# Post-norm decoder of two layers: the transfer of the shift rows moved from SP's instruction row to ScalarE's

## Chip, cores and metric

The kernel runs on one core of one Trainium2 chip. The metric is the device time of one execution in microseconds; the time of a kernel is the median of its runs. Three runs of the kernel before gave 3743.16, 3737.08 and 3737.75 us, so the median is 3737.75.

## The reference

Two decoder layers, each with `x = layernorm(x + f(x))` three times, for 16 sequences of 256 tokens, 128 features, 16 heads of 8. Layer 0 has self-attention, cross-attention to a context of 1601 keys of 96 features, and a mixture of experts. Layer 1 has a state-space layer, the same cross-attention with other weights, and a feed-forward net. The part that matters here is attention:

```python
scores = jnp.einsum('bqhd,bkhd->bhqk', q, k) * scale
weights = jax.nn.softmax(scores, axis=-1)
out = jnp.einsum('bhqk,bkhd->bqhd', weights, v).reshape(B, Lq, D)
return out @ w_o + b_o
```

## The kernel before

One function, `attention` (L158), builds each of the three attention stages (self, cross0, cross1); experts, the state-space layer and the feed-forward net stand between and after them. A program stage is written by hand for each engine, in one row of instructions per engine, and the engines meet through semaphores.

**Work of one batch.** Heads are taken in four quads of four heads (`g` 0 to 3). A product in full precision is made from bf16 parts: queries and keys are split into three bf16 parts each (`SPLIT_Q`, `SPLIT_K`, on GpSimd after the first batch, L277 to L283), and SP copies the parts, row by row, into stacked tiles `Q` and `K` (in self-attention one tile `QK`) by nine transfers at a time: `STACK_Q` (L348) once per batch, `STACK_K` (L361) once per quad in the cross stages, and once per batch in self-attention (L364). `LOAD_C` and `LOAD_X` (L333) fetch the inputs of a later batch.

For each quad the softmax needs the maximum of every query's scores first. TensorE computes scores for it (operation A, L486 and L493, into one of two ring buffers), VectorE takes the maxima (L663, L668, L672) into `nm`, GpSimd splits them in three bf16 parts (L407 to L413) into `mp`, TensorE transposes them (operation MT, L502), and ScalarE copies the transposed shift rows from PSUM to `mst` (L586, 32 x 256 bf16). Then one DMA, operation ROWS (L370), moves them as 64 short rows (16 KB) into the last rows of the stacked `Q` tile. There they take part in the second score product, so that exp gets the score less its maximum.

Operation B (L520) computes that product of scores, in slots of two units of two heads; ScalarE takes the exponentials (L600) into `Pr`; PV (L539) multiplies with the values into `oT`; after a quad, EV (L608) copies `oT` to `OTs`. At the end of a batch come the division (OX), two matmuls (ONT, OUT), and the layer norm. B of quad `g` begins with a wait for that quad's rows:

```python
if cp == 0 and pk == 0:
    pe.wait_ge(max_rows[g], 16 * (b + 1))
```

The score banks `sT` are three; B of a slot waits for the first exponential of the slot before it. GpSimd (before it writes `mp` again) and ScalarE (before it writes `mst` again) wait for the rows of the quad two before.

**The order of the work.** `_schedule` (L76) gives every operation a slot number, relative to its batch; `plan` sorts the operations of a pass by slot, then by rank (B, A, PV, MT, then all others), then by batch. Every engine walks through the same plan and issues what is its own, so each engine's order is fixed. A cross batch has 56 slots, 14 per quad (`u`); a self batch has 8, 2 per quad. In the cross stages:

```python
out += [(g * u - 4, ("MT", g)), (g * u - 3, ("ROWS", g))]
```

and in self-attention both stand in one slot, `g * u - 5`, MT first, and EV of the quad whose turn it is ahead of ROWS. In the cross stages the last two slots of a quad are short: they have one chunk of 65 keys in place of two chunks of 128. `STACK_K` for the next batch is scheduled at slots 27, 30, 44 and 57, `STACK_Q` at 12, `LOAD_C` at 27; the first of the `STACK_K` waits only for the split of the keys, the others also for the quad's last B.

On SP every operation stands behind the one ahead of it, so that a wait of one holds all that follow. ROWS waits there for ScalarE's copy: `read` (L133) gives the count of ScalarE's ring semaphore at which MT's buffer has been read. ScalarE's own row holds, per slot, the exponentials of B (two per slot), the copies of MT, EV, XT and ONT, and one issue of two DMAs for the feed-forward weights (`ffn_load`, L1455), behind the first XT of the second cross stage.

Of the kernel before, what the change touches and what calls it, by code (L numbers as in the profile page):

```python
# [13 lines left out]
P = 128  # L14
B, S, D = 16, 256, 128
H, DH = 16, 8
# [10 lines left out]
ROWS = P // 2  # L27
PASSES = (((0, 0), (0, 1), (1, 0), (1, 1), (0, 2)), ((2, 0), (1, 2), (2, 1), (2, 2)))
SHIFT = len(PASSES[1])
# [128 lines left out]
def attention(nc, top, cfg, X, ident_f, ident_b, src_T, wts, x_dram=None, ffn_weights=None):  # L158

    n = cfg.name  # L160
    with ExitStack() as ctx:
        def sb(name, shape, dt):
            return ctx.enter_context(nc.sbuf_tensor(f"{n}_{name}", shape, dt))
# [4 lines left out]
        def sem(name):  # L168
            return top.enter_context(nc.semaphore(f"{n}_{name}"))
# [19 lines left out]
        if cfg.cross:  # L189
            qparts = sb("qparts", [D, PARTS, S], BF16)  # L190
            kparts = sb("kparts", [D, PARTS, NKP], BF16)
            Qs = [sb(f"Q{j}", [P, PAIRS, 2, S], BF16) for j in range(cfg.qbufs)]
            Ks = [sb(f"K{j}", [P, PAIRS, 2, NKP], BF16) for j in range(cfg.kbufs)]
        else:
# [3 lines left out]
            Qs, Ks = ([T[:, :, :, k, :].rearrange("p t a n -> p a t n") for T in stacks] for k in range(2))  # L198
# [6 lines left out]
        mst = sb("mst", [2 * DH * 2, 2, S], BF16)  # L205
# [26 lines left out]
        by = {"dve": sem("ring_dve"), "act": sem("ring_act")}  # L232
# [6 lines left out]
        max_rows = [sem(f"max_rows{g}") for g in range(QUADS)]  # L239
# [18 lines left out]
        def rows(c):  # L258
            return cfg.chunks[c][1]
# [56 lines left out]
        @block.sync  # L316
        def _(sp):

            for dst, w in ((wq, "wq"), (wk, "wk"), (wv, "wv"), (wo, "wo")):
                n_in = wts[w].shape[0] // 16 * 16  # L320
                sp.dma_start(dst[0:n_in, :], wts[w][0:n_in]).then_inc(w_loaded, 16)
                if n_in < wts[w].shape[0]:
                    sp.dma_start(dst[n_in:, :], wts[w][n_in:]).then_inc(w_loaded, 16)
            sp.dma_start(bq[:, :], wts["bq"].rearrange("(p o) -> p o", o=1)).then_inc(w_loaded, 16)
            sp.dma_start(bo[:, :], wts["bo"].partition_broadcast(P)).then_inc(w_loaded, 16)

            for i in iterations:
                for op, ix, off in cfg.plan(i):
                    b = i + off
                    if op in ("LOAD_X", "LOAD_C"):  # L330
                        if b >= 2:
                            sp.wait_ge(by["dve"], cfg.read(i, "V", (len(cfg.chunk_units) - 1,), off - 2))
                        sp.dma_start(sT_in[b % 2][0:KIN, :], src_T[b]).then_inc(in_ready[b % 2], 16)  # L333
                        if x_dram is not None and b < 2:
                            n = NT // 2
                            sp.dma_start(X[:, b * n:(b + 1) * n, :],
                                         x_dram.rearrange("b (t p) f -> p (b t) f", p=P)[:, b * n:(b + 1) * n, :])\
                              .then_inc(x_in, 16)
                    elif op == "STACK_Q":
                        if b == 0:  # L340
                            sp.wait_ge(rows_set, cfg.qbufs)
                        if b >= cfg.qbufs:
                            sp.wait_ge(scored, NB * (b - cfg.qbufs + 1))
                        sp.wait_ge(split_q, SQ * (b + 1))
                        Q = Qs[b % cfg.qbufs]
                        for t, pairs in enumerate(PASSES):
                            for r, (a, _) in enumerate(pairs):
                                sp.dma_start(Q[r:P:DH, :, t, :], qparts[:, a, :]).then_inc(stacked_q, 16)  # L348
                    elif op == "STACK_K":
                        g = ix[0]  # L350
                        if b == 0:
                            sp.wait_ge(rows_set, cfg.qbufs + cfg.kbufs)

                        if b >= cfg.kbufs and not (cfg.cross and g == 0):
                            sp.wait_ge(scored, NB * (b - cfg.kbufs) + NB // cfg.kgroups * (g + 1))
                        if g == 0:
                            sp.wait_ge(split_k, SK * (b + 1))
                        for t, pairs in enumerate(PASSES):
                            for r, (qa, ka) in enumerate(pairs):
                                if cfg.cross:  # L360
                                    sp.dma_start(Ks[0][r:P:DH, g * KG:(g + 1) * KG, t, 0:NK],  # L361
                                                 kparts[g * KP:(g + 1) * KP, ka, 0:NK]).then_inc(stacked_k[g], 16)
                                else:
                                    sp.dma_start(stacks[b % cfg.kbufs][r:P:DH, t, :, :, :],  # L364
                                                 parts[:, qa:PARTS + ka + 1:PARTS + ka - qa, :])\
                                      .then_inc(stacked_k[0], 16)
                    elif op == "ROWS":
                        g = ix[0]
                        sp.wait_ge(by["act"], cfg.read(i, "MT", (g,), off))
                        sp.dma_start(Qs[b % cfg.qbufs][SHIFT:P:DH, 2 * g:2 * g + 2, 1, :], mst[:, g % 2, :])\  # L370
                          .then_inc(max_rows[g], 16)

        @block.gpsimd
        def _(pool):
# [190 lines left out]
        @block.scalar  # L565
        def _(act):
            act.wait_ge(w_ready, READY)

            for i in iterations:
                k = 0  # L570
                for op, ix, off in cfg.plan(i):
                    b = i + off
                    if op in cfg.reader:
                        R = ring[:, cfg.parity(i, k), :]
                        if cfg.reader[op] == "act":
                            act.wait_ge(filled, cfg.base(i, None) + k + 1)
                        k += 1
                    if op == "XT":
                        act.activation(xT[:, :], R[:, 0:S], ACT.Copy).then_inc(by["act"], 1)
                        if ffn_weights is not None and b == 0:  # L580
                            ffn_load(ffn_weights, act)
                    elif op == "MT":
                        g = ix[0]
                        if b * QUADS + g >= 2:
                            act.wait_ge(max_rows[(g + 2) % QUADS], 16 * (b + g // 2))
                        act.activation(mst[:, g % 2, :], R[0:4 * DH, 0:P].bitcast(BF16), ACT.Copy)\  # L586
                           .then_inc(by["act"], 1)
                    elif op == "B":
                        g, cp, pk = ix
                        for j in range(2):  # L590
                            u = g * UQ + 4 * cp + 2 * pk + j
                            act.wait_ge(scored, b * NB + u + 1)
                            if b * NB + u >= NPR:
                                was = (u - NPR) % NB
                                last = min(was % UQ // 4 * 2 + 1, NCHK - 1)
                                done = was // UQ * NV + 1 + [last in cs for cs in cfg.bursts].index(True)
                                act.wait_ge(weighed, b * NW + done - (NW if u < NPR else 0))
                            nc_ = min(2, NCHK - 2 * cp)
                            r = rows(2 * cp)
                            act.activation(Pr[0:r, u % NPR, 0:nc_ * S], sT[0:r, cfg.sT_bank(b, u), 0:nc_ * S],  # L600
                                           ACT.Exp).then_inc(exped, 1)
                    elif op == "EV":
                        g = ix[0]
                        gq = b * QUADS + g
                        act.wait_ge(weighed, (gq + 1) * NV)
                        if b > 0:
                            act.wait_ge(by["dve"], cfg.read(i, "OX", (g // 2,), off - 1))
                        act.activation(OTs[:, g, :], oT[:, 0:S], ACT.Copy).then_inc(o_out, 1)  # L608
                    elif op == "ONT":
                        act.activation(OnT[:, :], R[:, 0:S], ACT.Copy).then_inc(by["act"], 1)  # L610
# [844 lines left out]
def ffn_load(fw, act):  # L1455
    weights, lora = fw.dram
    act.dma_start(fw.raw[:, :, :], weights).then_inc(fw.loaded, 16)
    act.dma_start(fw.lora[:, :], lora).then_inc(fw.lora_loaded, 16)
# [270 lines left out]
```

## Time and profile before

| What | Value |
|---|---|
| Median of three runs | 3737.75 us |
| Profiled execution, its own time | 3738.05 us |
| Its span in the profile | 3736.1 us |
| Busy: PE, DVE, ACT, POOL | 3416.9, 2878.3, 2312.5, 1182.9 us |
| ROWS transfers | 64 in self-attention, 128 in the two cross stages |
| Self-attention | to about 330 us of the span |
| Cross stages | about 330 to 1732 us and 2260 to 3661 us |

PE is TensorE's matmul row, PEld its weight loads, DVE VectorE, ACT ScalarE, POOL GpSimd, SP the sync engine. A name with a q behind it, as SPq or ACTq, is that engine's instruction sequencer, where DMA issues stand; the time of such an issue is the time that it holds the sequencer, and its landing is counted from the start of the issue until its semaphore is full. In a timeline a row gives start and duration in us, engine, line, operation, output and inputs, and in brackets the idle time ahead of it with what ended it. Neighbouring instructions of a group are merged to one row, with their number behind the x.

### The profile page before, as it was taken

How to read it: one execution, taken by the hardware profiler on the slowest of the kernel's cores; microseconds unless marked ns; L12 is line 12 of the kernel's file. 1: busy time of each engine (PE TensorE's matmuls, PEld its weight loads, DVE VectorE, ACT ScalarE, POOL GpSimd, SP SyncE). 2: the span in 40 equal slices, each digit the busy share in tenths (PEclk: the TensorE clock that was granted, in tenths of full speed). 3: DMA queues.
4: the chain of work that ended last, by engine and by line, in shares of the span. 5: the costliest groups of instructions: out<-in, count | busy, mean ns of one | idle time of the engine just before them, and what ended most of it. 6: DMA issues, size and time to landing. Idle time of an engine off the chain costs nothing. (4 is left out here: it accounts for less than half of the span.)

```text
span 3736.1 us, 96496 instructions
## 1 busy us (share of the span) xinstructions
PE 3416.9 (91%) x38874; PEld 1684.4 (45%) x38874; DVE 2878.3 (77%) x3902; ACT 2312.5 (62%) x4560; POOL 1182.9 (32%) x1918
## 2 busy tenths in 40 slices
PE   6885999999999999998999684999999999999998
PEld 3442444444444444445676582444444444444445
DVE  5776788888888888885644996888888888888874
ACT  3663677777777767675333531677777777677773
POOL 5552222232222222212765263332222222332202
PEclk9997999999999999998999896999999999999999
DMA  4222222222322222220000002222322222222310
GB/s 102 76 74 68 55 63 57 57 59 56 71 66 65 55 63 57 56 47 27 1 1 2 1 1 69 61 56 62 75 59 62 55 65 55 61 56 61 69 22 24
DMA packets 159093, 195.26 MB, mean 52 GB/s; under 512 B 31268, under 2 KB 117288, under 8 KB 158392
## 3 DMA queue, kind: packets, MB, share of 16 engines
q1 hardware_dynamic: 158472, 188.49, 21.4%
q8 instruction: 307, 5.03, 0.6%
q14 instruction: 138, 1.13, 0.1%
q10 hardware_dynamic: 176, 0.61, 0.1%
HBM read 27.95 MB, written 2.10 MB: 8 GB/s over the span
## 5 line engine op out<-in xcount | busy, mean ns | idle before, releaser
L600 ACT ACTIVATE cross_Pr<-cross_sT 128x512 f32<-128x512 f32 (+1 forms) x3584 | 1833.6, 563 | 766.7 <-PE cross_sT L520 765.7
L663 DVE TENSOR_REDUCE cross_nm<-cross_ring 128x2 f32<-128x802 f32 x2048 | 1975.0, 991 | 321.1 <-PE cross_ring L486 292.6
L520 PE MATMUL cross_sT<-cross_Q,cross_K 64*128 64x256 bf16 x13312 | 1043.4, 273 | 47.8 <-ACT cross_Pr L600 42.1
L539 PE MATMUL cross_oT<-cross_Pr,cross_V 128*9 128x256 f32 x13312 | 1030.3, 381 | 0.0
L520 PEld LDWEIGHTS cross_sT<-cross_Q,cross_K 64*128 64x128 bf16 x13312 | 511.4, 95 | 769.1 <-ACT cross_Pr L600 636.7
L486 PE MATMUL cross_ring<-cross_K,cross_Q 64*128 64x401 bf16 x4096 | 661.9, 336 | 62.5 <-DMA cross_K<-cross_kparts 33.5
L407 POOL TENSOR_TENSOR cross_mp<-cross_nm,cross_one 128x8 bf16<-128x8 f32 x128 | 25.9, 202 | 1371.8 <-DVE cross_nm L668 1371.8
L539 PEld LDWEIGHTS cross_oT<-cross_Pr,cross_V 128*9 128x9 f32 x13312 | 198.2, 88 | 412.2 <-issue 245.7
L486 PEld LDWEIGHTS cross_ring<-cross_K,cross_Q 64*128 64x128 bf16 x4096 | 199.1, 94 | 203.2 <-DVE cross_nm L663 107.5
L967 ACT ACTIVATE moe_r<-moe_bank 128x512 f32<-128x512 f32 x144 | 85.9, 597 | 188.6 <-PE moe_bank L894 187.2
L857 POOL TENSOR_TENSOR moe_hh<-moe_r,moe_rc 128x512 f32<-128x512 f32 x128 | 169.1, 1326 | 88.2 <-DVE moe_rc L1089 87.5
L600 ACT ACTIVATE self_Pr<-self_sT 128x512 f32<-128x512 f32 x256 | 138.8, 594 | 85.0 <-PE self_sT L520 84.7
L672 DVE TENSOR_REDUCE self_nm<-self_ring 128x4 f32<-128x1024 f32 x128 | 155.3, 1223 | 46.7 <-PE self_ring L493 44.0
L1089 DVE TENSOR_TENSOR moe_rc<-moe_r,moe_bank 128x512 f32<-128x512 f32 x128 | 87.5, 686 | 131.0 <-PE moe_bank L907 130.4
L917 PEld LDWEIGHTS moe_bank<-moe_down,moe_hh 128*128 128x128 f32 x1152 | 150.6, 192 | 54.4 <-issue 40.8
L1245 PE MATMUL ssm_bank<-ssm_diag,ssm_state 128*128 128x128 f32 x1024 | 130.9, 291 | 46.4 <-DVE ssm_state L1366 46.4
L277 POOL TENSOR_TENSOR cross_qparts<-cross_qf,cross_one 128x256 bf16<-128x256 f32 x30 | 18.4, 612 | 485.2 <-DVE cross_qf L640 485.2
L917 PE MATMUL moe_bank<-moe_down,moe_hh 128*128 128x128 f32 x1152 | 152.6, 275 | 1.4 <-POOL moe_hh L857 1.2
L894 PE MATMUL moe_bank<-moe_xT,moe_up 128*128 128x512 f32 x288 | 148.5, 600 | 1.0 <-ACT moe_s L949 1.0
L1366 DVE TENSOR_TENSOR_SCAN ssm_state<-ssm_decay,ssm_dtu 128x2048 f32<-128x2048 f32 x32 | 145.8, 4603 | 4.5 <-ACT ssm_decay L1293 4.4
L1245 PEld LDWEIGHTS ssm_bank<-ssm_diag,ssm_state 128*128 128x128 f32 x1024 | 125.7, 204 | 51.5 <-DVE ssm_state L1366 51.4
L470 PE MATMUL cross_ring<-cross_wv,cross_in 97*128 97x128 f32 (+1 forms) x832 | 124.1, 296 | 21.0 <-DVE cross_nm L663 21.0
(272 smaller groups left out, 3075.2 us busy)
## 6 DMA issues: line engine op xcount, KB each, us to landing
cross_K<-cross_kparts SPq DMA_DIRECT2D x1152, 100.1 KB, 2.3
cross_in<-in_ctx_T_dram SPq DMA_DIRECT2D x32, 600.4 KB, 5.6
self_QK<-self_parts SPq DMA_DIRECT2D x144, 128.0 KB, 2.8
cross_Q<-cross_qparts SPq DMA_DIRECT2D x288, 64.0 KB, 2.1
self_in<-in_x_T_dram SPq DMA_DIRECT2D x16, 128.0 KB, 2.2
cross_Q<-cross_mst SPq DMA_DIRECT2D x128, 16.0 KB, 1.8
out_dram<-X SPq DMA_DIRECT2D x8, 256.0 KB, 2.3
moe_up<-in_moe_up_dram SPq DMA_DIRECT2D x1, 1152.0 KB, 6.0
```

The costliest lines, as they stand in the source:

```text
L470: mm = pe.matmul(R[0:r, (c - lo) * D:(c - lo + 1) * D], sT_in[b % 2][:, s:s + r], wv[:, :], start=True, stop=True)
L486: mm = pe.matmul(R[:, 512 * j:512 * j + cfg.block], Q[ROWS * j:ROWS * (j + 1), pair, 0, t * P:(t + 1) * P], K[ROWS * j:ROWS * (j + 1), pai ...
L520: mm = pe.matmul(sT[0:r, cfg.sT_bank(b, u + j), (c % 2) * S:(c % 2 + 1) * S], K[ROWS * j:ROWS * (j + 1), pair, t, s:s + r], Q[ROWS * j:ROW ...
L539: mm = pe.matmul(oT[32 * j:32 * j + VR, 0:S], V[0:r, b % VB, c, 4 * g + j, :], Pr[0:r, slot, (c % 2) * S:(c % 2 + 1) * S], start=(c == 0), ...
L600: act.activation(Pr[0:r, u % NPR, 0:nc_ * S], sT[0:r, cfg.sT_bank(b, u), 0:nc_ * S], ACT.Exp).then_inc(exped, 1)
L663: dve.tensor_reduce(nm4[:, g % 2, t, :, pk, blk], R.rearrange("p (j n) -> p j n", j=2)[:, :, 0:cfg.block], AX.X, ALU.max, negate=True).the ...
L672: dve.tensor_reduce(nm[:, g % 2, :, :, a].rearrange("p t j -> p j t"), R.rearrange("p (j t n) -> p j t n", j=2, t=QT), AX.X, ALU.max, nega ...
L857: pool.tensor_tensor(hh[:, s, :], r[:, s, :], rc[:, s, :], ALU.mult).then_inc(hidden, 1)
L894: pe.matmul(bank[:, n % UPS, :], up[:, m, :], xT[:, i * BLK:(i + 1) * BLK], start=True, stop=True)\
L917: mm = pe.matmul(bank[:, 5 + i % 2, t * D:(t + 1) * D], hh[:, n % BUFS, t * P:(t + 1) * P], down[:, m, :], start=(first and t == 0), stop= ...
L1245: return pe.matmul(bank[:, tile // BT, (tile % BT) * D:(tile % BT + 1) * D], lhs, rhs, start=first and tile % BT == 0, stop=True, skip_gro ...
L1366: dve.tensor_tensor_scan(state[:, k % BUFS, :], decay[:, k % BUFS, :], dtu[:, h * HALF:(h + 1) * HALF], 0.0, ALU.mult, ALU.add).then_inc(s ...
```

## The change

ROWS is taken out of SP's program and put into ScalarE's, at the same place of the same plan, with the same wait, semaphore, source and destination. Nothing else changes.

```diff
--- before.py
+++ after.py
@@ -364,11 +364,6 @@
                                     sp.dma_start(stacks[b % cfg.kbufs][r:P:DH, t, :, :, :],
                                                  parts[:, qa:PARTS + ka + 1:PARTS + ka - qa, :])\
                                       .then_inc(stacked_k[0], 16)
-                    elif op == "ROWS":
-                        g = ix[0]
-                        sp.wait_ge(by["act"], cfg.read(i, "MT", (g,), off))
-                        sp.dma_start(Qs[b % cfg.qbufs][SHIFT:P:DH, 2 * g:2 * g + 2, 1, :], mst[:, g % 2, :])\
-                          .then_inc(max_rows[g], 16)
 
@@ -585,6 +580,11 @@
                         act.activation(mst[:, g % 2, :], R[0:4 * DH, 0:P].bitcast(BF16), ACT.Copy)\
                            .then_inc(by["act"], 1)
+                    elif op == "ROWS":
+                        g = ix[0]
+                        act.wait_ge(by["act"], cfg.read(i, "MT", (g,), off))
+                        act.dma_start(Qs[b % cfg.qbufs][SHIFT:P:DH, 2 * g:2 * g + 2, 1, :], mst[:, g % 2, :])\
+                           .then_inc(max_rows[g], 16)
                     elif op == "B":
```

## Rows read from the trace of the kernel before

**Rows 1.** The page, busy us of each engine, share of the span and instructions.

```profile
PE 3416.9 (91%) x38874; PEld 1684.4 (45%) x38874; DVE 2878.3 (77%) x3902; ACT 2312.5 (62%) x4560; POOL 1182.9 (32%) x1918
```

**Rows 2.** Busy time by stretch: self-attention, and 470 us of cross0.

```profile
30.00:320.00 290.00, 237.07 (x2958) 134.61 (x2958) 204.51 (x339) 178.67 (x396) 144.25 (x410) 1.00 0.29 72
...
430.00:900.00 470.00, 456.81 (x5719) 197.70 (x5715) 389.57 (x490) 335.99 (x684) 110.12 (x204) 1.00 0.28 64
```

**Rows 3.** Timeline, cross0: two long slots in a row.

```profile
1028.94 0.61 PE L520 MATMUL cross_sT<-cross_Q,cross_K 64*128 64x256 bf16 x8
...
1029.59 1.08 ACT L600 ACTIVATE cross_Pr<-cross_sT 128x512 f32<-128x512 f32 x2 [0.21 <-PE cross_sT L520]
...
1030.24 0.61 PE L520 MATMUL cross_sT<-cross_Q,cross_K 64*128 64x256 bf16 x8
```

**Rows 4.** Timeline, cross0: around the ROWS of quad 2, short slots behind it.

```profile
1016.08 0.56 SPq L370 DMA_DIRECT2D cross_Q<-cross_mst  x1
1016.22 1.08 ACT L600 ACTIVATE cross_Pr<-cross_sT 128x512 f32<-128x512 f32 x2 [0.17 <-PE cross_sT L520]
...
1017.53 0.65 ACT L600 ACTIVATE cross_Pr<-cross_sT 65x256 f32<-65x256 f32 x2 [0.22 <-PE cross_sT L520]
...
1018.14 0.41 PE L520 MATMUL cross_sT<-cross_Q,cross_K 64*65 64x256 bf16 x4
...
1019.20 0.61 PE L520 MATMUL cross_sT<-cross_Q,cross_K 64*128 64x256 bf16 x8
```

**Rows 5.** Waits, 60 to 300 us: engine, line, waited for, us, times, longest.

```profile
ACT self_Pr L600 <- PE self_sT L520: 78.1, 64, 2.2
...
PE self_sT L520 <- ACT self_Pr L600: 6.5, 14, 0.5
```

**Rows 6.** ROWS by its tile and line: duration in ns, who waited, landing.

```profile
L370 SPq DMA_DIRECT2D cross_Q<-cross_mst x128: 539/540/563, 381.8 to 3633.9; - x128
...
  POOL self_mp L407: 76.2, 14
  PEld cross_sT L520: 6.0, 9
  PE cross_sT L520: 1.6, 5
...
DMA to landing us min/median/max: 1.7/1.8/3.7
```

**Rows 7.** Timeline, start of self-attention: a transpose MT.

```profile
54.24 0.27 PE L502 MATMUL self_ring<-ident_b,self_mp 128*32 128x128 bf16 x2 [0.88 <-POOL self_mp L413]
```

**Rows 8.** Timeline, start of cross1: a DMA issue behind a copy on ScalarE.

```profile
2267.78 0.38 ACT L579 ACTIVATE cross_xT<-cross_ring 128x256 f32<-128x256 f32 x1 [35.78 <-PE cross_ring L448]
2267.80 0.38 ACTq L1457 DMA_DIRECT2D ffn_raw<-in_L_ffn_weights_T_dram  x1
```

**Rows 9.** Timeline, self-attention: around one ROWS.

```profile
150.21 0.54 SPq L370 DMA_DIRECT2D self_QK<-self_mst  x1
...
150.35 1.08 ACT L600 ACTIVATE self_Pr<-self_sT 128x512 f32<-128x512 f32 x2
...
151.00 0.61 PE L520 MATMUL self_sT<-self_QK 64*128 64x256 bf16 x8 [0.47 <-ACT self_Pr L600]
...
151.76 1.05 PE L539 MATMUL self_oT<-self_Pr,self_V 128*9 128x256 f32 x16
...
153.11 0.29 PE L502 MATMUL self_ring<-ident_b,self_mp 128*32 128x128 bf16 x2 [0.29 <-DVE self_nm L672]
```

**Rows 10.** Last key split, SP's stack and load behind it; landings before, behind the load.

```profile
1009.93 0.30 POOL L283 TENSOR_TENSOR cross_kparts<-cross_res,cross_kparts 128x65 bf16<-128x65 f32 x1
...
1023.57 0.59 SPq L333 DMA_DIRECT2D cross_in<-in_ctx_T_dram  x1
...
cross_K<-cross_kparts SPq DMA_DIRECT2D x9, 100.1 KB, 2.3
...
cross_K<-cross_kparts SPq DMA_DIRECT2D x9, 100.1 KB, 4.2
```

## Prediction, made before the changed kernel was run

> **What bounds the kernel now.** Start with the page's busy line and the table by stage. TensorE is busy for 91% of the span, yet it isn't the whole story: in the first cross-attention stage, 430 to 900 us, PE, DVE and ACT are busy 457, 390 and 336 of 470 us [rows 1, 2]. Busy PE time is modelled, so the bound has to be read from the order of instructions. The timeline of one quiet slot shows a loop. The score matmuls (B) take 0.61 us. ScalarE starts two exponentials 0.04 us after their end, 1.08 us for the two. The next B starts 1.30 us after the one before, about 0.11 us after the first exponential ends. The sum 0.61 + 0.04 + 0.54 + 0.11 is 1.30 [rows 3]. So it is this handoff between PE and ACT that sets the time of a long slot. ScalarE has 0.21 us of idle time in each slot, before its next first exponential; a delay of ScalarE below that costs nothing, and one above it goes straight into the loop. The two slots after the one with ROWS are short (65 keys). The exponentials at 1017.53 last 0.65 us for two, so the first ends at 1017.86; with the same 0.11 us B could start at 1017.97, but it starts at 1018.14 [rows 4]. There PE has something else to finish, and ScalarE has 0.17 us more to spare.
>
> The stage of self-attention is looser: PE, DVE and ACT are busy 237, 205 and 179 of 290 us, and ScalarE waits for PE far more often than PE for ScalarE: from 60 to 300 us it is 78.1 against 6.5 us, and of these last waits there is about one per batch (14 in this stretch) [rows 2, 5].
>
> **What the change moves.** ROWS is one DMA of 16 KB per quad: 64 in self-attention, 128 in the two cross stages. Each holds SP for 0.54 us and lands 1.8 us after its issue. Waits of others for it: POOL 76.2 us, but PE only 6.0 us before weight loads and 1.6 us before matmuls [rows 6]. After the change the same 192 issues stand in ScalarE's own row, each behind a wait for ScalarE's own copy; nothing is computed less.
>
> **Gain on SP.** In self-attention one ROWS per batch sits behind nine stack transfers, and the POOL split, which waits for an earlier row to land, loses 76.2 us so, in 14 waits [rows 6]. But POOL is ahead of need: from 60 to 300 us no wait of PE for the POOL split stands in the list of waits, in which PE's 6.5 us for ScalarE do [rows 5]. Where nobody waits, its end is worth nothing. In the start-up a late row does reach PE: the transpose MT waits 0.88 us for the split [rows 7]. I take 0.9 us. In the cross stages, PE's waits on the rows are 7.6 us in all, in single places where a landing takes up to 3.7 us against a median of 1.8 [rows 6]. A different issuer has no reason to cure those; I take 0, with 7.6 us as the bound, so that the gain ends near 9 us.
>
> **Cost on ScalarE, cross stages (128 issues).** No row shows ROWS on ScalarE; the nearest is the load of the FFN weights. There ScalarE's copy starts at 2267.78 and lasts 0.38 us, and the DMA issue behind it starts at 2267.80 and takes 0.38 us [rows 8]. So the issue starts 0.02 us after the activation ahead of it has started, and runs beside it. ROWS is one slot after MT, so its wait is long fulfilled. Put it behind the second exponential of its slot: pair at 1016.22, second at about 1016.76, issue 1016.78 to 1017.32 (0.54, SP's duration for this shape), while the exponential ends at 1017.30 and the next is not due before 1017.53 [rows 4]. That leaves 0.21 us in which ScalarE must be ready again, and 0.17 us in the short slot behind it. Cost 0. If that cover failed, each 0.1 us beyond it would be 128 x 0.1 = 13 us.
>
> **Cost in self-attention (64 issues).** Here ROWS stands in MT's own slot, so ScalarE must wait until its copy is through. SP, which waits for the same copy, issues at 150.21, and at 150.35 ScalarE's next exponentials start [rows 9]. On ScalarE the issue would run from 150.21 to 150.75 and push those exponentials by 0.40 us. Queued behind the issue: the exponentials; waiting for them: B at 151.00, where PE waits 0.47 us now. This wait stands about once per batch. At the other quads ScalarE waits for PE, on average 78.1 / 64 = 1.2 us [rows 5], and the same 0.40 us vanish in it. B goes to 151.40 and PV from 151.76 to 152.16, ending at 153.21 instead of 152.81; MT, released at 153.11 by DVE, is late by 0.10 us [rows 9]. I take 16 x 0.10 = 1.6 us. Ends: nothing, or all 64 x 0.40 = 26 us.
>
> **Rows land later.** In the cross stages SP issues at 1016.08, ScalarE at 1016.78, and B of the next quad starts at 1019.20 [rows 4]: 2.42 us against a landing of 1.8, a reserve of 0.6 us, and no wait. SP changes too. The nine stack transfers of keys for the next batch, now held behind ROWS until 1016.64, depend only on the last POOL split, done at 1010.23. They would run from 1010.3 to 1016 or 1017, and the context load, now at 1023.57, would follow at once, in the same microsecond as ScalarE's ROWS [rows 4, 10]. What a load does to a neighbour: keys that land in 2.3 us land in 4.2 us right behind it [rows 10], 1.9 us more. That is behind it in one queue. If ROWS paid the whole of it, it would miss B by 1.9 - 0.6 = 1.3 us, in one quad of each of some 30 batches: 39 us. As ROWS is in another queue and small, I take 0 and keep 39 as the bound. The Trainium skill (DMA: Bandwidth & Descriptors, Queues, rings and completion order) says that each DMA engine takes turns between its queues packet by packet; by that ROWS waits for single packets of the load and not for its end. No row here shows two busy queues at once.
>
> **The sum.** -0.9 (start-up) + 1.6 (self-attention) + 0 + 0 = about +1 us on the profiled execution, 3738.05 us (span 3736.1 and 1.95 around it), which stands 0.3 us above the median of 3737.75. That gives 3739 us, no change. A measurement of this kernel can tell some 0.2%, 7.5 us.
>
> **Rival 1, slower: the issue isn't hidden.** The next exponentials would start only after the issue, and the issue after the second exponential's end, or take longer on ScalarE. Against it speaks the pair at 2267.78 [rows 8]; for it, that no activation follows there that would show when ScalarE is ready again. Place: the slot of ROWS. Price: issue from 1017.30 to 1017.84, next exponentials 0.3 us late, 0.1 to 0.3 us of it left after the short slot, x128 = 13 to 38 us; in self-attention 16 x 0.5 = 8 us. Time 3760 to 3785, middle 3772. It decides from an issue over 0.75 us, or as soon as ScalarE needs over 0.2 us to resume.
>
> **Rival 2, slower: self-attention doesn't absorb.** The 0.40 us count at more quads than one: 32 to 64 x 0.40 gives 13 to 26 us, 3751 to 3764. Against it: 78.1 us of ScalarE waiting for PE [rows 5].
>
> **Rival 3, slower: rows late beside the context load.** Up to 39 us as above; a half is more probable, 3758.
>
> **Rival 4, faster: SP was a bottleneck.** The 7.6 us of waits and the start-up's come back, and perhaps something of POOL's 76.2 us: 3729 to 3731. Against it: PE doesn't wait for those rows in any regular slot.
>
> That the change doesn't do what it says is improbable: the issue simply moves, and ACT's queue must show it.
>
> **Chances.** Forecast 0.60; rival 1 0.16; rival 2 0.06; rival 3 0.08; rival 4 0.10. Faster by over 0.2% 0.09, within 0.62, slower 0.29. Alone the forecast would have 3734 to 3745. For 8 in 10 the range reaches down to 3730 and up, into rival 1, to 3774.
>
> **What would show it.** Right: 192 DMA issues on ACT's queue of 0.54 us, starting 0.02 us after the second exponential; the gap after them at 0.2 us; 1.30 us slots; the wait of POOL on self_mst nearly gone; the keys' stack at 1010; landings of 1.8 to 2.4 us. Wrong: exponentials after ROWS that had been waiting for "issue" rather than PE (rival 1), PE L520 waiting on the rows' DMA once per batch (rival 3), or a cross stage whose first exponentials and maxima all come over 8 us later (rival 2).

## The result, and the profile after

Four runs of the changed kernel took 3790.85 to 3796.22 us, median 3791.72; four of the kernel before, beside them, 3737.08 to 3743.16, median 3738.44. The ratio is 1.0141, 95% interval 1.0129 to 1.0154: the change costs 53 us. The forecast was no change, 3739 us, and the range ended at 3774, so it was wrong in the time and in the range.

The profiled execution spans 3789.5 us (mean granted clock 0.964) against 3736.1 (0.973), 53.4 us more. From SP's first load of each stage, the stages became longer by 2.6 us (self-attention, its end at 330.2, now 332.8), 23.8 us (cross0, 1401.9 to 1425.7), 1.9 us (MoE and SSM), 25.9 us (cross1, 1401.1 to 1427.0) and -0.8 us (FFN). First the busy line and the queues of the page (columns of a queue: packets, MB, share of the 16 DMA engines):

```profile
PE 3436.7 (91%) x38874; PEld 1694.8 (45%) x38874; DVE 2879.0 (76%) x3902; ACT 2318.7 (61%) x4560; POOL 1183.1 (31%) x1918
...
q1 hardware_dynamic: 149256, 185.33, 20.8%
...
q10 hardware_dynamic: 9392, 3.76, 0.4%
```

The counts are those of [rows 1]. ACT's busy time has grown by 6 us of 3789, which excludes a slower ScalarE. PE's grew by 20 us with the same instructions, which asks for the clock. q10 is ScalarE's DMA queue and holds the rows now: the issue has moved as the diff says. Next comes ROWS by its tile: issue durations in ns (min/median/max), the engines that waited, in us and times, and the landing:

```profile
L586 ACTq DMA_DIRECT2D cross_Q<-cross_mst x128: 542/551/587, 384.4 to 3687.6; - x128
...
  PEld cross_sT L515: 46.8, 23
  PE cross_sT L515: 35.5, 18
...
DMA to landing us min/median/max: 1.7/1.8/6.1
```

Beside [rows 6], the issue and the median landing are as they were. But the longest landing went from 3.7 to 6.1 us, and PE's waits for the rows from 1.6 to 35.5 us. So it is a few transfers that are very late. The timeline shows one (waits in brackets):

```profile
1108.88 0.58 SPq L333 DMA_DIRECT2D cross_in<-in_ctx_T_dram  x1
1109.14 0.60 ACT L600 ACTIVATE cross_Pr<-cross_sT 128x512 f32<-128x512 f32 x1 [0.17 <-PE cross_sT L515]
1109.23 0.54 ACTq L586 DMA_DIRECT2D cross_Q<-cross_mst  x1
1109.63 0.59 ACT L600 ACTIVATE cross_Pr<-cross_sT 128x512 f32<-128x512 f32 x1
...
1110.45 0.65 ACT L600 ACTIVATE cross_Pr<-cross_sT 65x256 f32<-65x256 f32 x2 [0.22 <-PE cross_sT L515]
...
1114.36 0.61 PE L515 MATMUL cross_sT<-cross_Q,cross_K 64*128 64x256 bf16 x8 [2.17 <-DMA cross_Q<-cross_mst]
1115.00 1.08 ACT L600 ACTIVATE cross_Pr<-cross_sT 128x512 f32<-128x512 f32 x2 [2.85 <-PE cross_sT L515]
```

SP's context load is issued 0.35 us ahead of ROWS. The next long score matmul B stands still for 2.17 us, and behind it ScalarE for 2.85. The DMA view of 1108 to 1117 us gives KB each and microseconds to landing:

```profile
cross_in<-in_ctx_T_dram SPq DMA_DIRECT2D x1, 600.4 KB, 5.1
cross_Q<-cross_mst ACTq DMA_DIRECT2D x1, 16.0 KB, 5.1
```

16 KB on a queue of their own take as long as the 600 KB ahead of them. SP's own view tells how the load got there (start, time of all issues of the group):

```profile
1019.14 6.07 SPq L361 DMA_DIRECT2D cross_K<-cross_kparts  x9
1025.25 0.58 SPq L333 DMA_DIRECT2D cross_in<-in_ctx_T_dram  x1
...
1103.18 5.66 SPq L361 DMA_DIRECT2D cross_K<-cross_kparts  x9
1108.88 0.58 SPq L333 DMA_DIRECT2D cross_in<-in_ctx_T_dram  x1
```

In the kernel before, the same queue read:

```profile
1016.08 0.56 SPq L370 DMA_DIRECT2D cross_Q<-cross_mst  x1
1016.69 6.84 SPq L361 DMA_DIRECT2D cross_K<-cross_kparts  x9
1023.57 0.59 SPq L333 DMA_DIRECT2D cross_in<-in_ctx_T_dram  x1
```

There the nine stack transfers of keys came behind ROWS, and the load 7.5 us after it. Now nothing holds SP. The stack runs before ROWS, and the load falls within 0.9 us of it. When the stack takes 6.07 us, the load comes 0.05 us after ROWS (1025.20), and nothing is lost; when it takes 5.66, the load comes first. Of the 28 such loads in the two cross stages, 17 came first, by 0.06 to 0.36 us, and behind 15 of these ROWS was late: in the trace's DMA records its last piece ends 3.8 to 5.5 us after the issue, against 1.4 at an undisturbed one. At these 15 the matmuls of B stand still for 1.7 to 3.2 us, 34.7 of the 35.5 us in the list. (The landing above, 6.1 against 1.8, counts the semaphore too.) Behind the other two, keys still filled the DMA engines when the load came, and ROWS was not late.

Last, the clock. Below are two windows just after long stalls, at 1287.70 and 437.80, and the one that follows the first (columns: stretch, length, busy PE, PEld, DVE, ACT, POOL with counts, granted clock, DMA share, GB/s):

```profile
1287.70:1291.10 3.40, 3.40 (x30) 1.04 (x30) 1.23 (x2) 1.66 (x4) 0.00 (x0) 0.50 0.74 166
1291.10:1294.50 3.40, 3.06 (x46) 1.34 (x40) 2.99 (x4) 3.05 (x7) 0.00 (x0) 1.00 0.07 15
437.80:441.20 3.40, 3.40 (x30) 1.41 (x30) 1.46 (x2) 1.96 (x5) 0.00 (x0) 0.50 0.56 125
```

The granted clock is 0.50, the 1.2 GHz level: PE does 30 matmuls in 3.4 us in place of 46. Past the start of each stage there are nine such stretches of 3.41 us in the cross stages, each behind a late ROWS, where the kernel before has none. At a third to a half of 3.41 us lost in each (an estimate from 30 matmuls in place of 46, and from half the clock), they cost 11 to 15 us. PE's added waits are 35.5 - 1.6 = 33.9 us. Together that is 45 to 49 us of the 49.7 that the cross stages lost.

### The profile page after: what moved, and what is told of

Same layout as the page of the kernel before. It is cut to its first block and busy times, and to the rows that moved or that the text cites. A ratio compares the mean times of both kernels' runs of the same rounds, so it can differ in the third digit from the quotient of the medians.

```text
span 3789.5 us, 96496 instructions
## 1 busy us (share of the span) xinstructions
PE 3436.7 (91%) x38874; PEld 1694.8 (45%) x38874; DVE 2879.0 (76%) x3902; ACT 2318.7 (61%) x4560; POOL 1183.1 (31%) x1918
```

## The experiments

The theory: SP, no longer waiting at ROWS, moves the context load in front of ScalarE's ROWS, and ROWS then waits until the load is out. The rivals: ScalarE pays for the issues; self-attention; or something else that ScalarE's queue does to the rows. Unless a kernel is described otherwise, it is the changed kernel with the edit shown. The kernels did not all run on the same chip, so each is compared with its own runs of the kernel before.

**SP still waits, and issues nothing.** SP keeps the wait for ScalarE's copy in ROWS' place. The edit, against the kernel before; ScalarE's part is as in the change:

```diff
                     elif op == "ROWS":
-                        g = ix[0]
-                        sp.wait_ge(by["act"], cfg.read(i, "MT", (g,), off))
-                        sp.dma_start(Qs[b % cfg.qbufs][SHIFT:P:DH, 2 * g:2 * g + 2, 1, :], mst[:, g % 2, :])\
-                          .then_inc(max_rows[g], 16)
+                        sp.wait_ge(by["act"], cfg.read(i, "MT", (ix[0],), off))
```

> The changed kernel, in which SP keeps the wait for ScalarE's copy at the place of ROWS, but issues no ROWS (ScalarE does). Theory Q (the load is in the way: SP, freed of that wait, issues the context load just ahead of quad 2's ROWS, whose packets come only after the load's): the key stack starts after the copy again, the load follows some 7 us behind ROWS, the waits of PE L515 on cross_mst fall from 46.8 us to under 8, and the time is 3738 to 3743 us (before, plus about 2.6 us of self-attention). Theory I (the issue on ScalarE costs time by itself): the issues are all still there, so 3780 to 3795. Theory S (ScalarE's queue is slower for a small transfer whatever stands beside it): landings of quad 2 still 4 to 6 us in half of the batches, 3775 to 3795.

Measured: 3743.78 us (3740.96 to 3748.96), ratio 1.0012 [1.0002, 1.0021]. All but about 4 of the 53 us are back, though every ROWS is still ScalarE's. SP's queue, then the ACT and PE lines of one such slot:

```profile
1019.55 6.58 SPq L361 DMA_DIRECT2D cross_K<-cross_kparts  x9
1026.17 0.58 SPq L333 DMA_DIRECT2D cross_in<-in_ctx_T_dram  x1
```

```profile
1019.78 0.54 ACTq L588 DMA_DIRECT2D cross_Q<-cross_mst  x1
...
1022.67 0.61 PE L517 MATMUL cross_sT<-cross_Q,cross_K 64*128 64x256 bf16 x8
```

The load comes 6.4 us after ROWS, and B doesn't wait. Who waited for ROWS in the cross stages, over the whole run:

```profile
  PEld cross_sT L517: 9.1, 11
  PE cross_sT L517: 3.8, 6
```

So the issuing engine is not what costs; the order that SP's wait had kept is. The wait had held back both the key stack and the load; the next kernel moves the load alone.

**The load later in the plan.** One number in the planner:

```diff
-            out += [(-2 * s + 27, ("LOAD_C",))]
+            out += [(-2 * s + 33, ("LOAD_C",))]
```

> The changed kernel with one number of the schedule changed: LOAD_C at slot 33 instead of 27, so that SP issues the context load behind the second key stack and not behind the first. Theory Q: no load within 3 us of a ROWS; PE's waits on cross_mst under 8 us, 3738 to 3743 us. Theory I: 3780 to 3795, as changed. If only the key stack, now beside nothing, had been in the way (SP freed in general): still over 3765.

Measured: 3743.41 us (3740.11 to 3746.72), ratio 1.0008 [0.9999, 1.0018]; PE waits 2.1 us for the rows, the longest landing is 3.5 us. SP's queue:

```profile
1011.89 14.93 SPq L361 DMA_DIRECT2D cross_K<-cross_kparts  x18
1026.86 0.58 SPq L333 DMA_DIRECT2D cross_in<-in_ctx_T_dram  x1
```

Here the stack runs ahead of ROWS, as in the changed kernel, and does no harm. It is the load alone.

**The load held to the moment of the copy.** SP waits for the copy of quad 2 just before the load:

```diff
                             sp.wait_ge(by["dve"], cfg.read(i, "V", (len(cfg.chunk_units) - 1,), off - 2))
+                            if cfg.cross:
+                                sp.wait_ge(by["act"], cfg.read(i, "MT", (2,), 0))
```

> The changed kernel, with a wait in front of every context load for ScalarE's copy of quad 2 in the same pass, so that SP issues each load some 0.2 us ahead of ScalarE's ROWS. Theory Q: the loss stands in every batch with a load (28 to 30) instead of in 16: 28 x 2.7 = 76 us in place of 44, so 3738 + 2.6 + 76 = about 3817, 3805 to 3830; first packet of ROWS 2.8 us or more after its issue in each. Theory I: 3790 plus or minus 5, since the issues on ScalarE are the same. If engines took turns between queues in small packets, landings would stay under 2.6 us and the time under 3760.

Measured: 3797.02 us (3793.05 to 3804.07), ratio 1.0155 [1.0140, 1.0170], and not the 3817 of the theory. The premise was missed: in 12 of the 28 batches the stack was still being issued when the copy was through, and the load followed ROWS; in 16 it came ahead. ROWS was late in 15 batches, as many as in the changed kernel (where the expectation counts 16). PE's waits for the rows were 41.5 us in 18 places, and the span grew by 57.6 us, against 35.5 and 53.4. As the number of late ROWS is the same, this run doesn't tell the theories apart. Two kernels further down set that number.

**Self-attention alone.** ROWS is ScalarE's in self-attention, SP's in the cross stages. The edit, against the kernel before, in SP's row and in ScalarE's:

```diff
-                    elif op == "ROWS":
+                    elif op == "ROWS" and cfg.cross:
...
+                    elif op == "ROWS" and not cfg.cross:
+                        g = ix[0]
+                        act.wait_ge(by["act"], cfg.read(i, "MT", (g,), off))
```

> The kernel before, with ROWS issued by ScalarE in self-attention alone (64 of the 192). The first load of cross0 came 2.6 us later in the changed kernel. If that is the price of self-attention: 3738.4 + 2.6 = 3741, and PE's waits on cross_mst as before (under 8 us). If issues on ScalarE cost by themselves (theory I, 53 us over 192): 3738 + 18 = 3756.

Measured: 3741.69 us (3739.36 to 3748.17), ratio 1.0009 [0.9999, 1.0018]; its first load of cross0 stands at 332.87 us, 2.6 later than before. In the changed kernel the slot of [rows 9] reads:

```profile
150.58 0.55 ACTq L586 DMA_DIRECT2D self_QK<-self_mst  x1
151.24 1.09 ACT L600 ACTIVATE self_Pr<-self_sT 128x512 f32<-128x512 f32 x2 [0.42 <-issue]
151.89 0.61 PE L515 MATMUL self_sT<-self_QK 64*128 64x256 bf16 x8 [0.98 <-ACT self_Pr L600]
```

The exponentials wait 0.42 us for the issue, and B's wait has gone from 0.47 to 0.98. Its wait list from 60 to 300 us has it 15 times, once per batch as before:

```profile
PE self_sT L515 <- ACT self_Pr L600: 14.4, 15, 1.0
```

These waits were 6.5 us before [rows 5], so 7.9 us were added, and the stage became 2.6 us longer.

**Every load ahead of ROWS.** The kernel in which SP waits and issues nothing, with the load one slot earlier (26 for 27), where it stands right behind that wait:

```diff
-            out += [(-2 * s + 27, ("LOAD_C",))]
+            out += [(-2 * s + 26, ("LOAD_C",))]
```

> Hold (ScalarE issues ROWS, SP keeps the wait for the copy), with the context load at slot 26, ahead of the first key stack. SP then issues the load right after the copy of quad 2, about 0.2 us ahead of ScalarE's ROWS, in each of the 28 batches that have a load, with no stack in front of it. Theory Q (packets of ROWS come after the load's when the load was issued first, though the queues are two): first ROWS packet over 2.5 us after its issue and a wait of PE of 1.5 to 3 us in each of the 28; 28 x 2.4 = 67, so 3742 + 67 = about 3809, 3785 to 3830. If in the changed kernel the stack ahead of the load was what delayed ROWS, and not the load: landings stay under 2.6 us, 3742 to 3750.

Measured: 3833.93 us (3828.32 to 3842.61), ratio 1.0260 [1.0242, 1.0279]. One batch, and who waited over the run:

```profile
1039.91 0.32 SPq L333 DMA_DIRECT2D cross_in<-in_ctx_T_dram  x1
...
1040.14 0.56 ACTq L588 DMA_DIRECT2D cross_Q<-cross_mst  x1
...
1045.22 0.61 PE L517 MATMUL cross_sT<-cross_Q,cross_K 64*128 64x256 bf16 x8 [2.12 <-DMA cross_Q<-cross_mst]
```

```profile
  PEld cross_sT L517: 83.7, 32
  PE cross_sT L517: 67.8, 32
```

The load leads by 0.23 us. By the span it costs 3831.9 - 3742.3 = 89.6 us over the kernel in which SP waits and the load keeps its slot, 3.2 us for each of 28 loads. In the changed kernel the 49.7 us of the cross stages over 15 late ROWS were 3.3 each. One slot in the place of the load thus costs more than the whole change did, with the same issuer and the same instructions. The parts: 67.8 - 3.8 = 64.0 us of waits, and 16 stretches at 0.50 (54.6 us) that lose 19 to 27 us: 83 to 91. It is above the range expected, for the clock had not been counted.

**The same load in six pieces.** The same kernel, with each load in six transfers of 16 rows, so that each of the 16 DMA engines should get one row of a piece (in the records of the whole load its rows start in waves of 16); who waits for the load waits for all six:

```diff
-                        sp.dma_start(sT_in[b % 2][0:KIN, :], src_T[b]).then_inc(in_ready[b % 2], 16)
+                        for p in range(LP):
+                            n = KIN // LP
+                            sp.dma_start(sT_in[b % 2][p * n:(p + 1) * n, :], src_T[b][p * n:(p + 1) * n, :])\
+                              .then_inc(in_ready[b % 2], 16)
```

> Forced, with each context load issued as 6 transfers of 16 rows (one row for each DMA engine) in place of one of 96 rows (six for each). Bytes and rows are the same. If an engine finishes what one transfer has put in its queue before it turns to the other queue, ROWS now waits for one row of each engine: first packet under 2.0 us, landing under 2.6, time 3740 to 3752. If ROWS simply shares the rate with all bytes of the load in flight: first packet still over 2.5 us and 3785 us or more.

Measured: 3764.63 us (3762.01 to 3765.79), ratio 1.0072 [1.0057, 1.0087]: 69 of the 96 us are gone, with the same bytes, begun in the same place.

```profile
1024.01 2.94 SPq L336 DMA_DIRECT2D cross_in<-in_ctx_T_dram  x6
...
1024.24 0.54 ACTq L592 DMA_DIRECT2D cross_Q<-cross_mst  x1
...
1027.94 0.61 PE L521 MATMUL cross_sT<-cross_Q,cross_K 64*128 64x256 bf16 x8 [0.74 <-DMA cross_Q<-cross_mst]
```

The wait is 0.74 us in place of 2.12, and PE's sum is 21.4 us (27 waits) in place of 67.8. The span is 21.4 us over that of the kernel in which SP waits; 17.6 us more of PE waits and one stretch at 0.50 account for 19 of it. ROWS doesn't wait for all of the load then: in the DMA records 16 to 32 of its 96 rows start before ROWS does. In the batch shown the last piece of ROWS ends 2.06 us after its issue, but its semaphore is full only at 3.65; at an undisturbed one (1025.20 in the changed kernel) these are 1.42 and 1.92. So the wait that is left is mostly one for the semaphore, behind the data. But the pieces' issues are 0.5 us apart, so that five of six were issued after ROWS. This run doesn't tell whether the size of a piece or the pace of the issues does it.

**One queue for both.** The kernel before, where SP issues ROWS, with the load put right ahead of the ROWS of quad 2:

```diff
+                    if op == "LOAD_C" and i >= 0:
+                        continue
...
                         sp.wait_ge(by["act"], cfg.read(i, "MT", (g,), off))
+                        if cfg.cross and g == 2 and b + 2 < B:
+                            sp.wait_ge(by["dve"], cfg.read(i, "V", (len(cfg.chunk_units) - 1,), 0))
+                            sp.dma_start(sT_in[b % 2][0:KIN, :], src_T[b + 2]).then_inc(in_ready[b % 2], 16)
```

> The kernel before (ROWS on SP), but in the cross stages SP issues the context load for the batch after next right behind the wait for quad 2's copy and directly ahead of that quad's ROWS: load and ROWS in one queue, the load first. Theory Q holds that a queue of its own gave ROWS nothing: ROWS is issued some 0.65 us behind the load, its first packet comes when the load's are out (about 3 us after its issue), landing 3.5 to 4.5 us, that is at 0.65 + 4 = 4.7 us after the copy, against 3.1 us between the copy and B: 1.5 us in each of 28 batches, 42 us, about 3780 us (3765 to 3800). If the other queue had made it worse than one queue: under 3755.

Measured: 3820.20 us (3816.53 to 3822.25), ratio 1.0220 [1.0205, 1.0236].

```profile
1033.85 0.32 SPq L374 DMA_DIRECT2D cross_in<-in_ctx_T_dram  x1
...
1034.22 0.57 SPq L375 DMA_DIRECT2D cross_Q<-cross_mst  x1
...
1038.85 0.61 PE L525 MATMUL cross_sT<-cross_Q,cross_K 64*128 64x256 bf16 x8 [1.81 <-DMA cross_Q<-cross_mst]
```

ScalarE issues none of it, and the loss is there: 83 us. PE waits 62.0 us in 30 places, against 67.8 with two queues. A queue of its own gives a small transfer no way past a load that is already out.

**Does ScalarE pay for issues?** To the kernel in which SP waits, one or two transfers are added behind each ROWS of the cross stages. They copy the same 16 KB to a spare tile that nobody reads; this is added work. ScalarE's next copy of shift rows waits for them.

```diff
                            .then_inc(max_rows[g], 16)
+                        if cfg.cross:
+                            for e in range(EXTRA):
+                                act.dma_start(spare[:, g % 2, e, :], mst[:, g % 2, :]).then_inc(spared, 16)
```

With two:

> Hold, with two more copies of the shift rows (16 KB each, to a spare tile) issued by ScalarE behind every ROWS in the cross stages, 3 issues in a row: 0.09 + 0.55 + 0.6 + 0.6 = 1.84 us after the start of the slot's first exponential, while the next exponential is due at 1.30 us. Theory Q with a cover of 1.2 us (slot) and about 0.17 us more behind it: 1.84 - 1.30 - 0.17 = 0.4 us x 128 = 50 us over hold, 3790 us (3775 to 3815). If ScalarE's sequencer queued the next exponentials ahead of the issues, nothing: 3743. If each issue costs ScalarE by itself 53/192 = 0.28 us: 256 x 0.28 = 70 us, 3813.

Measured: 3809.27 us (3807.65 to 3816.28), ratio 1.0196 [1.0181, 1.0211]: 72 us over the kernel before, or 68 once the 4 us of the kernel without extras are taken off, 0.53 us per ROWS.

```profile
1034.09 0.57 ACTq L593 DMA_DIRECT2D cross_Q<-cross_mst  x1
...
1034.68 1.31 ACTq L597 DMA_DIRECT2D cross_spare<-cross_mst  x2
...
1036.09 0.65 ACT L610 ACTIVATE cross_Pr<-cross_sT 65x256 f32<-65x256 f32 x2 [1.01 <-PE cross_oT L539]
```

The three issues end at 1035.99, and the exponentials start at 1036.09. PE's matmuls never wait for the rows here and its weight loads 0.6 us in all, so this is the price of issues alone. And with one:

> Hold with one more copy of the shift rows behind every ROWS on ScalarE, where extra2 had two and came 66 us behind hold (0.51 us per ROWS of the cross stages). The two issues end 0.09 + 0.55 + 0.6 = 1.24 us after the start of the slot's first exponential, and the next is due at 1.30. If the cover is the slot and the short slot behind it, this costs nothing to 0.05 us each: 3742 to 3750. If extra issues cost in proportion, half of extra2's loss: 3742 + 33 = 3775.

Measured: 3750.99 us (3750.53 to 3753.39), ratio 1.0035 [1.0021, 1.0049], or 8 to 9 us over the kernel without extras, 0.07 us per ROWS.

```profile
1020.35 0.54 ACTq L593 DMA_DIRECT2D cross_Q<-cross_mst  x1
...
1020.92 0.69 ACTq L597 DMA_DIRECT2D cross_spare<-cross_mst  x1
1021.70 0.65 ACT L610 ACTIVATE cross_Pr<-cross_sT 65x256 f32<-65x256 f32 x2 [0.37 <-PE cross_sT L520]
```

With two issues (1.26 us) the exponentials start after an idle time of 0.37 us, against 0.22 with one, which is the idle time in [rows 4] too. The cover is thus about 1.2 us, and one ROWS of 0.54 us lies well inside it: what the single issue costs is nothing that the cross stages show.

**A version that might win.** ROWS is ScalarE's in the cross stages alone, with the load at slot 33; self-attention is as before. The edit is the planner's line above and the two conditions on `cfg.cross`, turned round.

> ROWS on ScalarE in the cross stages alone, with the context load at slot 33; in self-attention ROWS stays on SP. With the load out of the way and without self-attention's 2.6 us nothing of the changed kernel's 53 us should be left: 3736 to 3741, the same as before within 0.1%. It is also the candidate to be faster than both: by less than 2 us at most, since PE waits on the rows only where an instruction fetch delays them. If ScalarE's issues cost anything by themselves in the cross stages, 3745 or more.

Measured: 3739.94 us (3735.85 to 3742.49), ratio 1.0003 [0.9994, 1.0012]. With both costs removed the change is worth nothing. None of these versions beats the kernel before.

## Why the prediction was wrong

**The step that failed is "Rows land later"**, taken at 0 and bounded at 39 us. All its preconditions came true as written: SP's stack and load run ahead and the load falls in the same microsecond as ScalarE's ROWS. Three of its sizes did not hold.
- The weight. "As ROWS is in another queue and small, I take 0" was a reason without a row, as the text said itself: no row showed two busy queues at once. The run with one queue (62.0 us of waits) beside the one with two (67.8) shows that the other queue protects nothing. Rival 3, whose preconditions were all read from rows, had 0.08 and deserved far more.
- The price of one. The extra landing was taken from keys behind a load, 1.9 us [rows 10], giving a stall of 1.3. Measured: last pieces that end at 3.8 to 5.5 us against 1.4, and matmul stalls such as 2.17. The 15 stalls of PE are 2.3 us on average. The load lands in 5.1 us, and the rows land with it. Only the issue's earlier place, below, kept it from being worse.
- The count and the clock. Some 30 batches were assumed; 15 of 28 lost. And the granted clock falls after nine of the stalls, 11 to 15 us that the sum did not have. So 15 x 3.3 = 50 us in the cross stages, against 30 x 1.3 = 39. That the bound of 39 lies near 50 is luck: too many batches, at too low a price.

The Trainium skill (DMA: Bandwidth & Descriptors, Queues, rings and completion order) was read too kindly in the prediction. It says that a DMA engine changes queues only at the end of a packet, and that a packet holds typically 9 to 17 descriptors; the prediction took a packet for one row. The load is 96 rows over 16 engines, six per engine, so as an estimate from that page's figure all of an engine's share can be one packet, and ROWS would have to wait for it. The trace agrees: its DMA records of the 15 late ROWS show 74 to 94 of the load's 96 rows started before the first piece of ROWS. What the profile counts as a packet is a single row, so a bundle of rows can't be seen in it. The run in six pieces fits the page, but doesn't prove it.

**The issue hidden on ScalarE (0): right in its cost.** Two issues cost 0.07 us per ROWS and three 0.53, and the last version, with one, shows no cost (1.0003). The place was not: the issue was forecast 0.02 us after the second exponential's start; it starts 0.09 us after the first one's (1109.14 and 1109.23), and the second runs on time. So ROWS leaves half a microsecond earlier: 2.89 us before its B in the run where SP waits (1019.78 and 1022.67), against the 2.42 forecast. Rival 1 (13 to 38 us) is refuted.

**Self-attention (+1.6), start-up (-0.9): right in both terms, the end of the stage missing.** Forecast +0.7 together, measured +2.6. The push of the exponentials was forecast at 0.40 us and shows as 0.42; B waits longer by 0.51, once per batch. The transpose of [rows 7], at 54.24 before, starts 1.0 us earlier in the changed kernel:

```profile
53.24 0.28 PE L497 MATMUL self_ring<-ident_b,self_mp 128*32 128x128 bf16 x2
```

Of this, 0.4 us are left at the transpose at 62 us. From there to 310 us the transposes fall back, from 0.4 us ahead to 1.3 behind in some 14 batches: 0.12 us per batch, against 0.10 forecast. The last 1.3 us are lost after 310 us, at the end of the stage, for which the sum had no term; what takes them wasn't traced. Rival 2 (13 to 26 us) is refuted by the self-attention run.

**No gain on SP: right.** POOL's wait for the rows of self-attention fell from 76.2 us in 14 waits to 8.5 in 3, and the stage got no shorter. Rival 4 is refuted by the self-attention run (1.0009) and the last version (1.0003), which take SP's issues away in one kind of stage each.

**What remains open.** Why SP's nine stack transfers take 5.66 us in some batches and 6.0 or more in others; that decides on which side of ROWS the load falls, and so why 15 of 28 pay. About 4 us between the kernel in which SP waits and the kernel before are 2.6 from self-attention and the rest at the edge of what was measured. The 1 to 5 us of the cross stages beyond waits and clock aren't assigned. The runs also don't tell by what rule a DMA engine lets the load's rows go first: a bundle that it must finish, or the pace at which rows are issued to it.

## What to carry to other kernels

A DMA issue in a queue of its engine is also a gate: with it goes the wait in front of it, and all that stood behind it on that engine starts earlier. Before moving one, write down where each following transfer will start, and look for a large one that lands on a small one with little slack. A separate queue doesn't protect the small one; the order in time does, and it can be kept by a wait without an issue or by a later due time.

## What the hardware showed that was not expected

- 16 KB on ScalarE's queue, issued 0.06 to 0.36 us behind a 600 KB load on SP's queue, end after 3.8 to 5.5 us in place of 1.4, in 15 of 17 cases. In the other two the keys ahead of the load held up its first row until 2.0 and 2.5 us after its issue, and ROWS ended in 1.8 and 2.2 us. Issued 0.05 to 0.9 us ahead of the load, they end in 1.4 to 1.8 us; but in the run with the load held to the copy one ROWS issued 0.04 us ahead of its load was late too (5.8 us).
- ScalarE starts a DMA issue 0.09 us after the start of the first of two exponentials that stand ahead of it, and the second still follows without a gap (1109.14, 1109.63). About 1.2 us of issues per such pair are nearly free (0.07 us); three in a row (1.9 us) hold ScalarE up (0.53 us).
- After stalls of PE's matmuls of 1.9 to 3.2 us the granted clock was 0.50, the 1.2 GHz level, for 3.41 us: nine times in the changed kernel. Behind its other six late ROWS, with stalls of 1.7 to 2.3 us, it stayed at 1.00. It fell 16 times with every load ahead, and once with the load in pieces, whose stalls are short but for that one (1.95 us).
- In the kernel before, ROWS of the cross stages landed late (over 2 us, up to 3.7) 23 times of 128, and each time a 16 KB packet of the instruction queue (q8 on the page) moved between issue and landing; the 87 without such a packet landed in at most 1.81 us. These packets are not what makes ROWS late behind a load: with every load ahead, 13 of the 28 late ROWS have none.
